# Graph layer kernel: pick blocks one quad later, one register load for four window offsets, and two small vector operations placed between the window additions

## The reference, cut to what matters

```python
h = relu(layernorm(x))
s, v = h[:, :32] @ W_up_s / sqrt(32), einsum('nui,uw->nwi', h_v, W_up_v) / sqrt(32)
w0, w1, w2, w3 = split(silu(silu(edge_attr_8 @ A1 + b1) @ A2 + b2) @ A3, 4)
ss, vs = s[src], v[src];  y_s, y_v = edge_attr_4[:, :1], edge_attr_4[:, 1:4]
mji = concat([ss*y_s*w0, (vs . y_v)/sqrt(3)*w3, ss*y_v*w1, vs*y_s*w2])   # per edge
message = segment_sum(mji, dst, 6250) / 10.0
return x + concat([message_s @ W_out_s, message_v @ W_out_v]) / 8         # per node
```

## Time and profile before

| | us |
|---|---|
| median of 3 runs (range) | 1974.23 (1972.98 to 1976.07) |
| the profiled execution, own time | 1977.78 |
| its span in the trace | 1975.9 |
| PE busy | 1641.9 (83%) |
| POOL busy | 1424.3 (72%) |
| DVE busy | 1341.6 (68%) |
| ACT busy | 393.4 (20%) |

### The profile page before, as it was taken

How to read it: one execution, slowest core, us unless ns; L and a number is a source line. 1 busy time by engine, 2 the same in 40 slices (tenths; PEclk the granted TensorE clock), 3 DMA queues, 4 the chain that set the end, 5 groups by cost and what they waited for, 6 DMA issues and landing times. The chain is left out here.

```text
span 1975.9 us, 70774 instructions
## 1 busy us (share of the span) xinstructions
PE 1641.9 (83%) x22862; PEld 1276.1 (65%) x22862; DVE 1341.6 (68%) x2623; ACT 393.4 (20%) x640; POOL 1424.3 (72%) x1558
## 2 busy tenths in 40 slices
PE   5898788888887888788878887888888888888885
PEld 3676567666675676666656665766667667666674
DVE  4777667676676676766766766667667667676675
ACT  3212111121121112121211211111111111121121
POOL 4777777777777777777777777777777777777771
PEclk8899889898898898998988988989889889898897
DMA  8222222222222222222222222222222222222222
GB/s 238 63 67 63 69 68 62 65 71 64 64 68 65 67 64 67 69 62 64 71 58 68 61 66 67 60 63 71 59 65 63 66 67 61 61 72 60 63 66 82
DMA packets 127308, 137.78 MB, mean 70 GB/s; under 512 B 74780, under 2 KB 96853, under 8 KB 126679
## 3 DMA queue, kind: packets, MB, share of 16 engines
q0 software_dynamic: 48096, 97.92, 19.9%
q1 hardware_dynamic: 78134, 33.75, 6.7%
q10 hardware_dynamic: 576, 0.05, 0.0%
HBM read 125.14 MB, written 6.43 MB: 67 GB/s over the span
## 5 line engine op out<-in xcount | busy, mean ns | idle before, releaser
L625 POOL DMA_INDIRECT rows<-node_table,src_in x1491 | 1407.3, 944 | 493.8 <-issue 433.9
L905 PEld LDWEIGHTS pss<-tab_sb,x_sb 128*128 128x128 f32 x4704 | 598.2, 207 | 94.8 <-DVE x_sb L749 56.8
L905 PE MATMUL pss<-tab_sb,x_sb 128*128 128x128 f32 x4704 | 648.0, 295 | 0.0
L749 DVE TENSOR_TENSOR x_sb<-picks_in,psx 128x1024 f32<-128x1024 int32 (+1 forms) x294 | 364.1, 1240 | 214.0 <-PE pss L905 207.7
L872 PE MATMUL psw<-a_bd,h 64*128 64x128 f32 x3136 | 298.2, 311 | 109.4 <-DVE msgs L776 96.4
L776 DVE TENSOR_TENSOR msgs<-rows,psw 128x768 f32<-128x768 f32 x392 | 371.4, 947 | 0.0
L872 PEld LDWEIGHTS psw<-a_bd,h 64*128 64x128 f32 x3136 | 220.6, 198 | 184.8 <-DVE msgs L776 90.1
L893 PE MATMUL pss<-msgs,onehot 128*32 128x64 f32 (+1 forms) x12544 | 322.3, 248 | 0.0
L792 DVE TENSOR_TENSOR xT_sb<-xT_sb,psx 128x32 f32 x784 | 146.3, 187 | 247.0 <-DVE xT_sb L792 162.4
L893 PEld LDWEIGHTS pss<-msgs,onehot 128*32 128x32 f32 x12544 | 253.8, 116 | 52.4 <-issue 8.0
L774 DVE TENSOR_TENSOR msgs<-rows,psw 128x256 f32<-128x256 f32 x392 | 164.3, 419 | 130.2 <-PE psw L872 93.3
(11 more groups left out here) (67 smaller groups left out, 345.6 us busy)
## 6 DMA issues: line engine op xcount, KB each, us to landing
rows<-node_table SPq DMA_DIRECT2D x3072, 0.5 KB
rows<-node_table,src_in POOLq DMA_INDIRECT x1491
ef_in<-in_efT SPq DMA_DIRECT2D x100, 96.0 KB
picks_in<-in_picks SPq DMA_DIRECT2D x50, 64.0 KB
attr_in<-in_attr SPq DMA_DIRECT2D x100, 32.0 KB
xT_sb<-in_xT SPq DMA_DIRECT2D x7, 448.0 KB, 8.3
x_sb<-in_x SPq DMA_DIRECT2D x7, 448.0 KB, 8.0
out_T<-xT_sb SPq DMA_DIRECT2D x1, 3136.0 KB, 8.8
```

The source lines that it names most:

```text
L625: pool.indirect_dma_start(out=rows[:, quad_slot(p) + t, :], out_offset=None, in_=table, in_offset=bass.IndirectOffsetOnAxis(ap=src_in[:, b ...
L749: dve.tensor_tensor(pick[:, n, :], picks_in[:, i, :].unsqueeze(1).broadcast_to([P, nt, P]), node_ps[:, n].unsqueeze(2).broadcast_to([P, nt ...
L905: last = nc.tensor.matmul(pss[:, o % 2, CH:CH + F], pick[:, t, :], tab_sb[:, t, :], start=False, stop=(r % 2 == 1 and t == PICK_BLOCKS[r + ...
```

## The change

Three edits, all in DVE's program; the instructions of the other engines stay as they are, in the same order.

1. `pick_blocks` of step c moves from quad r = c + 1 of a half to quad r = c + 2 (`PICK_LAG` = 2), behind the messages of that quad as before. It waits for PE's use of step c, which in quad c + 2 lies two quads back instead of one. At r = 7 there is now a step before `scale`, at r = 1 none.
2. `load_starts` loads the four offsets of an oct with one register load ahead of the four additions; before there were four loads, each ahead of its addition.
3. `relative` and `equal` of the next oct stand between the additions (after the first and after the second), no longer behind the messages of the even quad. The additions still wait for one another.

```diff
--- before.py
+++ after.py
@@ -63,13 +63,14 @@
 SINGLE_PART = P // BODY
 PICKS = QB // RING
 PICK_STEPS = 6
+PICK_LAG = RING - PICK_STEPS
 PICK_BLOCKS = [NT * c // PICK_STEPS for c in range(PICK_STEPS + 1)]
 SLOTS = 2
 MSG_SLOTS = 4
 HOT_SLOTS = 4
 OCTS = QB // 2
 CH = 2 * F
-WINDOW_LAG = 2 * OW
+OUT_LAG = 2
 EPS = 1e-5
 MLP_HALF = HT * P // 2
 
@@ -778,16 +779,18 @@
                                           w[:, :, :, 1, :].unsqueeze(3).broadcast_to([P, QT, 2, 3, MUL]),
                                           ALU.mult).then_inc(msgs_ready, 1)
 
-                    def add_window(j, n):
-
-                        o, i = divmod(n, OW)
-                        (start,) = nc.values_load_multi_w_load_instructions(
-                            start_at[0:1, bass.ds(j * 2 * QB + n, 1)], engines=[mybir.EngineType.DVE],
+                    def load_starts(j, o):
+
+                        return nc.values_load_multi_w_load_instructions(
+                            start_at[0:1, bass.ds(j * 2 * QB + o * OW, OW)], engines=[mybir.EngineType.DVE],
                             min_val=0, max_val=NPAD,
                             skip_runtime_bounds_check_because="the round's first steps clamp the starts")[1]
+
+                    def add_window(j, o, i, start):
+
                         if i == 0:
                             dve.wait_ge(out_ready, j * OCTS + o + 1 + OUT_CREDIT)
-                        dve.wait_ge(window_added, j * 2 * QB + n + ADD_CREDIT)
+                        dve.wait_ge(window_added, j * 2 * QB + o * OW + i + ADD_CREDIT)
                         at = xT_sb[:, bass.ds(start, W)]
                         dve.tensor_tensor(at, at, pso[:, i * W:(i + 1) * W], ALU.add).then_inc(window_added, 1)
 
@@ -798,20 +801,26 @@
                             g = p // 2 + 1
                             half, r = divmod(p, RING)
                             ahead = (j + g // OCTS, g % OCTS) if not (last and 2 * g >= LAST_QUADS) else None
-                            n = 2 * p - WINDOW_LAG
-                            if p % 2 == 0 and not (first and n < 0):
-                                for i in range(OW):
-                                    add_window(j, n + i)
+                            o = p // 2 - OUT_LAG
+                            if p % 2 == 0 and not (first and o < 0):
+                                starts = load_starts(j, o)
+                                add_window(j, o, 0, starts[0])
+                            if ahead and p % 2 == 0:
+                                relative(*ahead)
+                            if p % 2 == 0 and not (first and o < 0):
+                                add_window(j, o, 1, starts[1])
+                            if ahead and p % 2 == 0:
+                                equal(*ahead)
+                            if p % 2 == 0 and not (first and o < 0):
+                                add_window(j, o, 2, starts[2])
+                                add_window(j, o, 3, starts[3])
                             if not last and r in (RING - 3, RING - 1):
                                 place_picked(j, half, (r - RING + 3) // 2)
                             messages(j, p, quad_tiles(p) if last else quad_gathers(p), not last and p == QB - 1)
-                            if not last and 1 <= r <= PICK_STEPS:
-                                dve.wait_ge(pick_used, (j * PICKS + half) * PICK_STEPS + r)
-                                pick_blocks(j * PICKS + half + 1, (half + 1) % 2, r - 1)
-                            if ahead and p % 2 == 0:
-                                relative(*ahead)
-                                equal(*ahead)
-                            elif ahead:
+                            if not last and r >= PICK_LAG:
+                                dve.wait_ge(pick_used, (j * PICKS + half) * PICK_STEPS + r - PICK_LAG + 1)
+                                pick_blocks(j * PICKS + half + 1, (half + 1) % 2, r - PICK_LAG)
+                            if ahead and p % 2 == 1:
                                 scale(*ahead)
 
                     relative(0, 0)
@@ -823,8 +832,10 @@
                     with dve.Fori(1, NJ - 1) as j:
                         iteration(j)
                     iteration(NJ - 1, last=True)
-                    for n in range(2 * LAST_QUADS - WINDOW_LAG, 2 * LAST_QUADS):
-                        add_window(NJ - 1, n)
+                    for o in range(LAST_OCTS - OUT_LAG, LAST_OCTS):
+                        starts = load_starts(NJ - 1, o)
+                        for i in range(OW):
+                            add_window(NJ - 1, o, i, starts[i])
 
                 @block.tensor
                 def _(pe):
```

## The result

The changed kernel takes 1971.68 us (1967.52 to 1975.31, 20 runs); the kernel before, run in turn with it, 1975.82 us. The ratio is 0.9978 [0.9972, 0.9985]: 0.2% faster, where 1.8% was forecast. The profiled execution took 1972.19 us, with a span of 1970.4.

A forecast was written before the change was run, and what follows sets the result against it. PE-DVE chain taken as the bound, gathers at 76.2 us beneath; 0.83 + 0.66 + 0.0 = 1.49 us an iteration, times 21.5 is 32.0, with (f) 35: median 1939 us, 8-in-10 range 1923 to 1957.

The forecast's parts named there:

- The bound: Whole loop: the chain PE-DVE sets the 78.43 us iteration; gathers allow no less than 76.2, so at most 2.2 to win.
- (a): Quads 3 to 5 and 11 to 13: PE's waits of 0.42 and 0.41 us go, 0.83 us won per iteration.
- (b): Quads 14 to 15: messages come 0.66 us earlier, PE's wait falls from 1.13 to 0.47; kept, the loop's turn costing nothing.
- (c): Quads 6 to 9: 0.66 us earlier messages and faster additions offset the added 1.26 us pick step; net 0.0.
- X: Time of the four additions with the small pair between them: forecast 1.5 us, from 1.3 to 2.1, against 2.09 before.
- (d): Additions reach their wait for `project` sooner, above all in quad 2; cost nothing.
- (e): SP asks for the next pick list one quad later, beside other work; no cost expected.
- (f): Last iteration: 2.5 of PE's 2.8 us wait for messages goes, plus 0.5 us of additions at the end.
- The two rivals that hung on X (2.5 and 3.3): Register load mildly in the way, X 2.5, 1961 us, chance 0.12; load and steps in series, X 3.3, 2007 us, 0.07.
- POOL becomes the bound: Rival: smaller X or PE's clock staying up longer brings the iteration to the gathers' 76.2 us; 1923 us, chance 0.13.
- Nothing changes: Rival: DVE's waits only move to the weights and PE is as late as before at all six places; 1974 us, chance 0.04.
- a third place where the clock falls: Sign of being wrong: PE's clock, which falls to half in two places of an iteration, falls in a third.

The follow-up runs named there:

- the lag alone: The kernel before with the pick steps one quad later and nothing else; 1974.88 us, 0.9999 of before.
- the kernel without the lag: The kernel before with the one register load for four offsets and the small operations between the additions, pick steps unmoved; 1941.29 us, 0.984 of before.
- 192 columns: The changed kernel with the 16 pick matmuls of quad 4 taking 192 columns instead of 128, also called the wide one; 1971.54 us, 0.9983 of before.
- the cut loop: The changed kernel with PE's loop body cut behind the begin of quad 1 instead of between quads 15 and 0; 1969.35 us, 0.9972 of before.
- before with its pause filled: The kernel before with one layer-1 matmul (two instructions) repeated in quad 8; 1975.27 us, 0.9999 of before.
- the filled kernel: The changed kernel with two layer-1 matmuls repeated in quad 8, 92 useless instructions in all; 1944.16 us, 0.9832 of before.

## Why the forecast was wrong, step by step

**The bound.** Right as far as it went: PE and DVE set the pace in before, and where they don't, the gathers do, near 76.2 us. PE's clock was no part of it.

**(a), quads 3 to 5 and 11 to 13.** Right. The waits of 0.42 and 0.41 are gone; -0.54 in the second stretch.

**(b), quads 14 and 15.** The wait of 1.13, forecast at 0.47, is 0.49 in this row:

```profile
1064.28 0.71 PE L883 MATMUL psw<-a_bd,h 64*128 64x128 f32 x8 [0.49 <-DVE msgs L777]
```

But "this one is kept" fell behind the loop's turn. The first stretch became 0.91 us longer with as much half clock as before, 10.2 us. It lies elsewhere. Over thirteen iterations of each, the clock before fell on average 0.8 us into PE's pause and rose 7.5 us behind the first matmul after it; now it falls 2.5 us into the pause and rises at 9.2. Some 1.7 us of half clock moved off an idle engine onto work, which takes twice its time there (weights 0.71 and 1.22 us): about 0.9 lost. The pauses alone, first of before, then of after:

```profile
1070.50:1073.90 3.40, 0.02 (x3) 0.00 (x0) 0.75 (x4) 0.38 (x1) 2.48 (x4) 0.59 0.24 61
```

```profile
1065.70:1069.30 3.60, 0.00 (x0) 0.00 (x0) 3.23 (x9) 0.38 (x1) 2.69 (x4) 0.83 0.25 62
```

A clock of 0.59 in the pause before, 0.83 after. That the shorter wait in quad 15 is what moved the fall fits the order of events, and no run tested it alone. It can't be the only thing: in the kernel with the lag alone this wait is 0.96 to 1.19 us, and of the same thirteen the clock falls 0.6 to 0.9 us behind the pause's begin in five and 3.7 to 4.0 behind it in eight.

**(c), quads 6 to 9: the step that failed.** Its sizes were right. The additions with the small pair take 1265.49 - 1264.23 = 1.26 us (X was put at 1.5); from the messages of quad 7 to those of quad 8 it is 1265.49 - 1260.63 = 4.86 us against 5.1 forecast; PE waits 0.52, 1.02 and 0.85 where 0.39, 1.2 and 0.85 were forecast. These rows show the additions:

```profile
1264.23 0.17 DVE L795 TENSOR_TENSOR xT_sb<-xT_sb,psx 128x32 f32 x1
1264.33 0.17 DVE L719 TENSOR_TENSOR rel<-dst_in,start_now 128x8 f32<-128x8 int32 x1
1264.54 0.19 DVE L795 TENSOR_TENSOR xT_sb<-xT_sb,psx 128x32 f32 x1
1264.65 0.43 DVE L727 TENSOR_TENSOR psx<-psx,rel 128x256 f32<-128x256 f32 x1
1264.99 0.50 DVE L795 TENSOR_TENSOR xT_sb<-xT_sb,psx 128x32 f32 x2
1265.49 0.42 DVE L775 TENSOR_TENSOR msgs<-rows,psw 128x256 f32<-128x256 f32 x1
```

"Nothing is won or lost here" was wrong all the same, in what a wait is worth. The clock fell in this stretch in before already, the sum priced its waits at their own length, and the half clock that they bring had no term. It grew from 4.6 to 6.8 us, +0.84. And what there was to win was never the 4.4 us of waits: without the fall this stretch is 3 us shorter with the same waits. Together with the 0.91 us behind the loop's turn in (b), where the sum had "cost nothing", this took back the 1.49 us that the sum counted on.

**(d), (e).** Nothing to see in either, as forecast.

**(f).** Wrong: in the last iteration PE waits 3.0 us for DVE's messages, as before (2.8), where 2.5 of them were to go. That this iteration is 2.0 us shorter goes with 8.9 us less of half clock.

**The register load.** Four offsets take 344 ns against 303 for one, where 0.47 us were worked out: 14 ns for each value more. The Trainium skill ("Runtime: NRT & Kernel Launch", Instruction fetch mechanics) gives about 200 ns for each register, by which it would be an estimated 0.8. It speaks there of the loads ahead of a program, and the loads here read from SBUF, so the two may not be the same case; for this one the measurement decides. The two rivals that hung on X (2.5 and 3.3) fell with it.

```profile
L784 DVEq TENSOR_LOAD <-start_at x196: 340/344/356, 68.3 to 1956.8; - x196
```

**The rivals.** "POOL becomes the bound" named the right lever, PE's clock with fewer pauses, and its mechanism is real, but not in this kernel: its place is the kernel without the lag. "Nothing changes" came nearest in time (1974), by luck: it wanted PE's own order to be the bound at all six places, and the waits at four of them did go or shrink. The last sentence of the prediction feared a third place where the clock falls. There is none; it stays down longer in one of the two, and begins later in the other. The range, 1923 to 1957, had no case in which the waits go and the clock takes their time back.

**What stays open.** Why the falls of the clock, and with them the iterations, come just 78.5 us apart: before, after and four variants of them (the lag alone, 192 columns, the cut loop, before with its pause filled) have iterations of this mean length, although their stretches differ by up to 2.4 us. And which pauses make the clock fall in quad 8: equal waits in quads 6 to 8 gave both outcomes in one kernel; 1.34 us of waits in sum (0.66 and 0.68) brought none in 22 iterations; and 0.60 in the filled kernel brought one. What else counts, the stretch before them for instance, no run here isolates.

## What to carry to other kernels

Where the granted clock moves in a loop, list it by stretch beside the waits before you sum anything: a wait beside which the clock falls can be worth several times its length (moving one DVE step took 1.2 us of waits and 4.0 us off the stretch here), and a shorter wait may only move the half clock from idle time onto work. Ask of a change not how much waiting it removes in total but whether it clears the one place where the clock falls; here the place of a DVE step of 1.26 us decided over 32 us. And measure the parts of a compound change apart: one half of this one was worth 1.6% by itself, and the other half took nearly all of it back.

## What the runs showed of the hardware

- With the same waits to a hundredth of a us, the clock falls in one iteration and not in another of the same kernel; a fall cost 2.99 us on a stretch of 13.82. The Trainium skill, "TensorE: Matmul & The Clock Gate", in the section on a second HAM failure mode, describes the like of it in another kernel, an engine that idles in small pieces between groups of matmuls and loses throughput to the clock's going back and forth. The traces agree that the clock goes back and forth with waits of 0.2 to 1.0 us, and show besides that the same waits may bring no fall.
- Useless matmuls in a pause can shorten a kernel: 92 instructions of them took 27 us off this one.
- In three traces (before, after and the wide one) the clock's falls at the loop's turn keep a distance of 78.5 us to a hundredth, while single iterations are up to 0.6 us shorter or longer.
- A register load costs DVE 303 ns for one value, 344 for four; SP's of 32 took 2062.
- The branch at the end of PE's loop leaves the engine idle for some 3.5 us when cut between quads 15 and 0, and for 1.7 to 1.9 when cut in quad 1. Two more matmuls in the body brought a new pause of 0.96 us at another place, for which the trace names no engine.
